# Weights fetched by ScalarE, additions of exponentials after the masks, and row work in order: a transformer block on one core

## What is computed

```python
def _L0_attn_ref(x, Wqkv, bqkv, Wo, bo):            # 16 heads of 32
    kqv = x @ Wqkv + bqkv
    scores = einsum('bsnh,btnh->bnst', k, q) / sqrt(32)   # triangular: half is masked
    attn = softmax(scores, axis=2)
    out = einsum('bnkq,bknh->bqnh', attn, v)
    return out @ Wo + bo
def _L0_ffn_ref(hidden, gate_w, ..., down_scale):   # int32 weights, less 128, times scales
    h = silu(hidden @ Wg.T) * (hidden @ Wu.T)
    return h @ Wd.T
x = x + _layernorm(_L0_attn_ref(_layernorm(x), Wqkv, bqkv, Wo, bo))
x = x + _layernorm(_L0_ffn_ref(_layernorm(x), gate_w, ..., down_scale))
```

## Time and profile before

| | us |
|---|---|
| runs, median of 3 | 1640.79 (1640.74 to 1642.38) |
| the profiled execution | 1639.89 |
| its span in the profile | 1638.1 |
| TensorE busy in the span | 1544.6 (94%) |
| VectorE, ScalarE, GpSimd busy | 939.4, 795.9, 592.7 |

### The profile page before, as it was taken

One profiled execution on the slowest core, in us unless ns is written; L12 is line 12 of the kernel. 1 busy time (PEld: TensorE's weight loads), 2 busy tenths in 40 slices (PEclk: granted clock), 3 DMA queues, 4 the chain that ended last, 5 costly groups with the idle time before them and its releaser, 6 DMA issues.

```text
span 1638.1 us, 24488 instructions
## 1 busy us (share of the span) xinstructions
PE 1544.6 (94%) x9322; PEld 641.2 (39%) x9324; DVE 939.4 (57%) x1864; ACT 795.9 (49%) x1284; POOL 592.7 (36%) x809
## 2 busy tenths in 40 slices
PE   4899999998999999999977999999999999999997
PEld 2333334333333333333322244444444444444443
DVE  5666755788756887667756333564434343434344
ACT  5356676667666776667755633232222222222222
POOL 4335664677556766755755310020000000000001
PEclk8999999999999999999988999999999999999999
DMA  4212322224411233223345431221111111111000
GB/s 181 92 50 52 77 55 53 67 64 117 105 48 35 81 106 88 61 52 95 106 137 164 108 97 45 59 97 38 47 26 52 26 52 26 52 26 52 1 26 26
DMA packets 113398, 112.26 MB, mean 69 GB/s; under 512 B 69632, under 2 KB 69632, under 8 KB 113024
## 3 DMA queue, kind: packets, MB, share of 16 engines
q1 hardware_dynamic: 113280, 110.69, 23.7%
HBM read 45.37 MB, written 25.17 MB: 43 GB/s over the span
## 4 chain that ended last, share of the span: by engine, by line
PE 72%; DVE 10%; POOL 6%; ACT 4%; issue 4%; SPq 3%; DMA 1%; POOLq 0%; ACTq 0%; DVEq 0%
PE ps L976 25%; PE ps L897 16%; PE ps L993 12%; PE ps L960 10%; PE ps L934 5%; DVE mcol L1255 4%; SPq L753 3%; POOL pt L1467 2%; PE ps L910 2%; ACT pt L1109 1%; POOL rs L1387 1%; PE ps L918 1%; DVE st L1150 1%; DVE xh L650 1%; POOL pt L1458 1%
## 5 line engine op out<-in xcount | busy, mean ns | idle before, releaser
L1109 ACT ACTIVATE pt<-ps,nrm 128x512 f32<-128x512 f32 (+1 forms) x640 | 361.5, 647 | 222.0 <-PE ps L934 208.8
L976 PE MATMUL ps<-x2in,gu 128*128 128x512 f16 x2048 | 462.4, 379 | 0.1
L1255 DVE TENSOR_REDUCE mcol<-ps 128x1 f32<-128x512 f32 (+2 forms) x636 | 318.0, 566 | 139.3 <-PE ps L918 93.1
L976 PEld LDWEIGHTS ps<-x2in,gu 128*128 128x128 f16 x2048 | 200.2, 98 | 242.0 <-ACT sg L1130 0.6
L1384 POOL TENSOR_SCALAR rs<-mv 128x1 f32<-128x1 f32 x120 | 27.2, 226 | 652.4 <-DVE mv L1154 646.1
L1326 DVE SCALAR_TENSOR_TENSOR hf<-ps,usc,sg 128x512 f32<-128x512 f32 x128 | 96.1, 751 | 259.1 <-PE ps L976 245.6
L1135 ACT ACTIVATE hh<-hf 128x512 f16<-128x512 f32 x128 | 80.7, 631 | 258.8 <-DVE hf L1326 245.2
L1467 POOL TENSOR_TENSOR pt<-pt 128x1024 f32<-128x1024 f32 x84 | 201.5, 2421 | 1.8 <-ACT pt L1109 1.8
L934 PE MATMUL ps<-qpack,kpack 98*128 98x512 f16 (+3 forms) x768 | 163.6, 331 | 29.0 <-DVE mcol L1255 25.7
L993 PE MATMUL ps<-wd,hh 128*128 128x512 f16 x496 | 188.0, 379 | 0.0
L993 PE MATMUL ps<-wd,hl 128*128 128x512 f16 x496 | 188.0, 379 | 0.0
(11 more groups left out here) (125 smaller groups left out, 1592.8 us busy)
## 6 DMA issues: line engine op xcount, KB each, us to landing
qpack<-stage SPq DMA_DIRECT2D x192, 64.0 KB, 2.0
kpack<-stage SPq DMA_DIRECT2D x192, 64.0 KB, 2.0
xr<-in_x SPq DMA_DIRECT2D x32, 256.0 KB, 2.9
x1d<-xr SPq DMA_DIRECT2D x32, 256.0 KB, 2.3
x2d<-xh SPq DMA_DIRECT2D x32, 256.0 KB, 2.3
x1in<-x1d SPq DMA_DIRECT2D x8, 1024.0 KB, 5.8
out_x<-yy SPq DMA_DIRECT2D x32, 256.0 KB, 2.0
xin<-in_x SPq DMA_DIRECT2D x24, 256.0 KB, 2.9
```

The lines of the kernel that those rows point to most:

```text
L976: mm = pe.matmul(bk, GU[:, c, m, i * 128:(i + 1) * 128], x2in[:, 1 - k, p, c, :], start=p == 0 and c == 0, stop=p == 1 and c == 3)
L1109: act.activation(Pt[:, PBUF[step], h, off:512], ps[:, BANK[job], off:512], ACT.Exp, scale=esc).then_inc(s_ex, 1)
L1255: mm = dve.tensor_reduce(mcol[:, n % 2, col:col + 1], scores, AX.X, ALU.max)
```

## The change

- **Additions.** Those of key block 3 (step 7) both come after the masks of key block 4; one of the two stood ahead of them.
- **Product with ones.** den(n, 1, 0) stands first in the products of step 0 of the next group, not last in step 9.
- **Projections of every third group** (n % 4 == 2): qk in steps 3, 5, 7, 9 (were 1, 3, 7, 9), the vproj of step 0 in step 1.
- **Rows in order.** A turn takes only the tile that was normalised first; in groups n % 4 == 1 no turn is placed in steps 5 to 7. By this, in groups 1, 2, 5, 6, 9 and 10 several stats, norms and turns stand in other steps. In step 3 and later dev jobs stand as before, in steps 0 to 2 all but the first come after the scores and their masks.
- **Fetches.** Weight blocks 1 to 7 are fetched by DMAs from ScalarE's list, each a step after the conversion of the block before.

```diff
--- before.py
+++ after.py
@@ -106,14 +106,14 @@
     b, g = divmod(n, 4)
     out = {}
     if n + 2 < NG:
-        for i, s in enumerate(((0, 2, 3, 7) if b else (1, 3, 7, 9), (0, 1, 2, 3), (1, 3, 7, 9), (1, 2, 3, 8))[g]):
+        for i, s in enumerate(((0, 2, 3, 7) if b else (1, 3, 7, 9), (0, 1, 2, 3), (3, 5, 7, 9), (1, 2, 3, 8))[g]):
             out[s] = ("qk", n + 2, i % 2, i // 2)
     if n == 0:
         for i, s in enumerate((0, 2, 5, 8)):
             out[s] = ("vproj", 4 + i)
     if b + 1 < B:
         first = 8 * b + 8 + (0, 0, 2, 7)[g]
-        for i, s in enumerate(((), (7, 9), (0, 2, 4, 6, 8), (0,))[g]):
+        for i, s in enumerate(((), (7, 9), (1, 2, 4, 6, 8), (0,))[g]):
             out[s] = ("vproj", first + i)
     if g == 3:
         for i, s in enumerate((5, 7, 9)):
@@ -147,7 +147,7 @@
         if g == 1 and b + 1 < B:
             chains += [(NS * n + (0, 1, 2, 3, 4, 5, 6, 7)[k], LN1, 8 * b + 8 + k) for k in range(8)]
     at = {}
-    untaken = 0
+    untaken = []
 
     def free(kind, step):
 
@@ -163,14 +163,19 @@
             kind = kinds[0]
             if kind == "residual" and ("wo_stats", t - 2) in at and at.get(("turn2", t - 2), step) >= step:
                 continue
-            if kind == "residual" and adding(step):
+            if adding(step) and (kind == "residual" or step // NS % 4 == 1 and kind in ("ln1_turn", "turn2")):
                 continue
             if kind == "ln1_stats" and t >= 10 and at.get(("ln1_norm", t - 2), step) + 2 > step:
                 continue
-            if kind in ("ln1_norm", "norm2") and untaken == 2 or kind in cost and not free(kind, step) and (
-                    room.get(step, 99) < cost[kind]):
+            if kind in ("ln1_norm", "norm2") and len(untaken) == 2 or (
+                    kind in ("ln1_turn", "turn2") and untaken[0] != t):
                 continue
-            untaken += {"ln1_norm": 1, "norm2": 1, "ln1_turn": -1, "turn2": -1}.get(kind, 0)
+            if kind in cost and not free(kind, step) and room.get(step, 99) < cost[kind]:
+                continue
+            if kind in ("ln1_norm", "norm2"):
+                untaken.append(t)
+            if kind in ("ln1_turn", "turn2"):
+                untaken.pop(0)
             if kind in cost and step in room and not free(kind, step):
                 room[step] -= cost[kind]
             at[kind, t] = step
@@ -186,9 +191,9 @@
     summed = step[0] < SUMS and step[1] == 1 and step[2] < 4
     out = [] if summed else [("den",) + step]
     out.append(("num",) + step)
-    if summed and step[2] > 0:
-        out += [("sum",) + step + (h,) for h in (0, 2) if h == 0 or s != 7]
-    return out + [("den", n, 1, 0)] * (s == NS - 1 and n < SUMS)
+    if summed and step[2] in (1, 2):
+        out += [("sum",) + step + (h,) for h in (0, 2)]
+    return [("den",) + step[:2] + (0,)] * (s == 0 and step[0] < SUMS) + out
 
 
 
@@ -241,7 +246,10 @@
         for s, (j, kb) in enumerate(STEPS):
             here = rows.get(NS * n + s, [])
             add(("step", n, s))
-            plan += [("dev", DEV_FOR[job[0]], job[1]) for job in here if job[0] in DEV_FOR]
+            plan += [("act_fetch", i) for i in range(1, 8) if ffn_step(i - 1) + 1 == NS * n + s]
+            devs = [("dev", DEV_FOR[job[0]], job[1]) for job in here if job[0] in DEV_FOR]
+            soon = 1 if s < 3 else len(devs)
+            plan += devs[:soon]
             lot, of = (s + EARLY, n + 1) if s < NS - EARLY else (s + EARLY - NS, n + 2)
             if of < NG:
                 add(("mjob", of, lot))
@@ -251,11 +259,11 @@
             products = products_of(pend, n, s)
             if n < NG - 2:
                 plan += products
-            plan += [("score", n, j, kb, h) for h in range(4)]
+            plan += [("score", n, j, kb, h) for h in range(4)] + devs[soon:]
             if n < NG - 2 and pend is not None and last(*pend[1:]):
                 plan += [("invert",) + pend[:2], ("normalise",) + pend[:2]]
             if s == 7 and n < NG - 2:
-                add(("sum",) + pend + (2,))
+                plan += [("sum",) + pend + (h,) for h in (0, 2)]
             if s == NS - EARLY and n + 1 < NG:
                 plan += [("mjoin", n + 1), ("mturn", n + 1)]
             if n >= NG - 2:
@@ -274,7 +282,7 @@
             if n == NG - 3 and s == NS - 2:
                 plan += [("ffn_fetch", 10)]
             plan += [each for i in range(24) if ffn_step(i) == NS * n + s
-                     for each in [("ffn_load", i)] + [("ffn_fetch", k) for k in range(24) if RAW_BEFORE[k] == i]]
+                     for each in [("ffn_load", i)] + [("ffn_fetch", k) for k in range(8, 24) if RAW_BEFORE[k] == i]]
             pend = (n, j, kb)
         if n + 2 < NG:
             add(("packs", n + 2))
@@ -1108,6 +1116,11 @@
                     e.wait_ge(s_sc, NO[job])
                     act.activation(Pt[:, PBUF[step], h, off:512], ps[:, BANK[job], off:512], ACT.Exp, scale=esc
                                    ).then_inc(s_ex, 1)
+                elif kind == "act_fetch":
+                    i = a[0]
+                    e.wait_ge(s_cv["act"], i)
+                    ra, src, _ = raw_of_ffn(i)
+                    act.dma_start(ra, src).then_inc(d_raw[RAW[i]], 16)
                 elif kind == "ffn_load" and BY[a[0]] == "act":
                     i = a[0]
                     if FFN[i][0] == 4:
```

## The result

The changed kernel is slower: **1678.48 us** in the median of four runs (1674.40 to 1680.93), beside 1640.76 for the kernel before in the same runs (1636.63 to 1642.38). The ratio is 1.0231, with a 95% interval of 1.0203 to 1.026. The forecast was 1658 with a range up to 1667: the direction was right, the size was not. Of 37.7 us it named 17.5. The measured time is 11 us above the range.

The account below looks back on a forecast made before the run. TensorE's work was taken to set the pace, so the change could only add or remove waits. Terms -3.5 - 1.8 - 0.6 + 0.7 + 26.4 - 3.7 = +17.5 us gave 1658 us, range 1646 to 1667 (8 in 10).

Parts of the forecast that it names:

- masks ahead of one addition: Mask waits of TensorE shrink: -3.5 us for groups 4, 8 and 12, -1.8 in group 13, -0.6 in group 1.
- dev jobs after the masks: Steps 0 to 2: nothing for steps 5.3 and 9.3 (bound -2 us each), 0.8 us of gain in step 2.3.
- product with ones a step later: 8 matmuls, about 1.0 us, moved within TensorE past one set of scores: 0, at worst +0.3 us a group.
- row work and projections: Pairs of groups 5 and 6, 9 and 10 lose 13.2 us each, +26.4 together; group 2 gives +0.7.
- fetches on ScalarE: Without the fetch in SP's queue the wait in step 13.2 shrinks from 9.60 us to about 6: -3.7 (0 to -5).
- The stand: TensorE waits 15.2 us at step 6.2 (likewise 10.2) for masks behind a late turn; O is step 6.0's start.
- the half clock: After the long wait at step 6.2, likewise in groups 9 and 10, TensorE runs at half clock: +3.2 us a pair.
- Turns out of steps 5 to 7: Groups 5 and 9: masks and exponentials of step 5.8 come earlier, -3.3 us each (bounds -1 and -5.5).
- Rival 3: Worse: the wait sets off others, 4 us more in each pair and no gain from the fetches: 1670 us; chance 0.11.
- Rival 2: Comes out even: larger gains in groups 4, 5, 8, 9, 12, 13, clock costs 1: +2, 1643 us; chance 0.09.

Follow-up runs that it names:

- b_rows: The kernel before, with only the row work in order and the projections of groups 2, 6 and 10 as in the kernel after: 1664.52 us, +24.

## Why the prediction was wrong

It priced the new order of the additions as a gain and looked only at TensorE's masks and at the exponentials. The wait came at VectorE instead. The prediction had named this as a sign that it would be wrong: TensorE's wait "at another place, such as the additions in steps 7 and 8".

Each part alone, beside its term:

| part | forecast | alone on the kernel before |
|---|---|---|
| masks ahead of one addition | -5.9 | +7.9 |
| dev jobs after the masks | 0 | +5.7 |
| product with ones a step later | 0 | +1.6 |
| row work and projections | +27.1 | +23.9 |
| fetches on ScalarE | -3.7 | +0.3 |
| sum | +17.5 | +39.4, measured together +37.7 |

The +27.1 for row work holds a gain of 0.8 us in group 2 that the prediction gave to the dev jobs.

- **"Masks ahead of one addition": wrong, and the largest miss (13.8 us).** The wait for masks went, as said. The failed step is the sentence that the additions end as late as before and only the exponentials of step 8 wait for them. The last addition ended 5.1 us after the scores of step 3.7 and now ends 7.0 us after them; VectorE's maximum falls beside them and TensorE is behind it. And groups 0, 2, 3, 6, 7, 10 and 11, for which the prediction wrote "nothing", are changed as well: in the kernel after, groups 2, 3, 7 and 11 wait 1.3 to 1.6 us each at this maximum, where they had next to none. In all, TensorE waits 21.8 us for it, where it waited 2.6. The Trainium skill states the mechanism (SBUF — State Buffer, Who interferes with whom): a VectorE instruction with two SBUF inputs contends with a GpSimd instruction that reads SBUF, by an exclusive lock, and a reduction never does. The traces agree on each count: 0.17 us alone and up to 2.31 beside an addition, 0.188 at most as a reduction.
- **"dev jobs after the masks": wrong (5.7 us).** The prediction said that what ScalarE does just before waits for those dev jobs, now later, and then counted nothing for it. The trace of after has that wait (1.32 us in step 4.3), and it comes out at TensorE one step on.
- **"Fetches": the wait right, the rest of the term wrong.** The wait behind the copies shrank, by 4.3 us, more than forecast. The fetches on ScalarE, taken at 0 with a bound of 2.7, delay it by 0.63 us each where something stands ready behind them; the "each a step after the conversion of the block before" of the description of the change leaves out that on ScalarE's list fetch and conversion are neighbours. Most of what was lost again lies in stretches at half clock. The rule of the Trainium skill that the prediction cites (DMA: Bandwidth & Descriptors, Issuing engines are not separate DMA queues), by which another issuer brings next to nothing, gave the better number for the whole. But the runs show a gain at the wait and a loss elsewhere, not the absence of both.
- **The stand: right in mechanism and place, too large by some 3 us a pair.** A pair of groups loses 10.1 and 10.8 us in b_rows, where the prediction had 13.2. Cast, landing (issued at 442.94, landed 3.3 later at 446.24, O + 20.4 against O + 21) and release were right within 0.9 us. TensorE came there later than forecast: steps 6.0 and 6.1 took 11.7 us, not 9.8, since without a projection TensorE waits for exponentials and their masks instead (0.83 and 0.50 in step 6.1). And the half clock cost about 1.4, not 3.2: from arrival at O + 12.5 to release are 12.5 us of the 13.9 by which step 6.2 grew. 3.2 had been read where TensorE had a whole projection to do.
- **Turns out of steps 5 to 7: right.** 3.1 and 2.7 us in b_rows against 3.3; the 2.9 us of group 1 were not counted. In the kernel after it is spent on steps 5.2 and 5.4 (dev jobs, +1.0 and +1.2) and on step 5.8, where VectorE's subtraction for turn2(5) is held up by the additions and takes 2.63 us (0.68 alone).
- **The product with ones: nearly right.** Step 9 gives back only 0.2 of its 0.9 us in groups 3, 7 and 11, where TensorE did it while waiting.
- **The rivals** named none of this. Rival 3 had its 4 us more in the pair; the loss lay outside the pair. Rival 2 has a slip in its sum: the upper bounds for groups 4, 8, 12 and 13 add 0.5 and 0.9 us to what was taken, 1.4 and not 2.7, so its total is +3.3.

Left open: what lets the short stretches at half clock fall where they fall (steps 5.9, 6.1 or 9.3, from kernel to kernel). Each is worth some 1.6 us, and they blur comparisons of parts below 3 us.

## What to carry to other kernels

When an edit moves a long GpSimd instruction in time, list every VectorE instruction that will now run beside it and has two operands in SBUF, short ones above all, and ask who waits for it: 0.17 us can become 2.3, and writing it as a reduction took the conflict away here without moving anything. A duration that varies for one form of instruction (0.17 to 1.42 us in the kernel before) is the sign to look for. A block of DMA issues in one queue is a wall for whatever is behind it; moving the wall finds the next victim, cutting it in pieces between the steps removes it, here 13 us on the old kernel and 33 on the new. And before a wait is priced as gone, look at the next thing on that engine's list: here it was another wait of nearly the same length.

## What was not expected of the hardware

- VectorE's two-operand instruction beside a GpSimd addition doesn't slow down, it stands until the addition has ended: 0.17 us became 1.72 and ended with it. The larger subtraction for the lower half (0.68 us alone) took 2.63 in step 5.8 and ended 0.56 us after the second addition, about its own length, with four reductions just before it, over one operand from PSUM, at their usual pace:

```profile
412.77 4.67 POOL L1480 TENSOR_TENSOR pt<-pt 128x1024 f32<-128x1024 f32 x2
...
413.50 1.95 DVE L1268 TENSOR_REDUCE mcol<-ps 128x1 f32<-128x384 f32 x4 [2.14 <-PE ps L926]
...
415.37 2.63 DVE L658 TENSOR_TENSOR xh<-xn,xh 128x512 f16<-128x512 f32 x1
```

- A DMA issued by ScalarE directly behind the instruction that it waits for delays the next one by 0.63 us, of which the row shows 0.43 (0.37 or 0.38 in the others): the two instructions around it no longer overlap.
